# First self-attention of a two-layer decoder: the attention result is added to x by GpSimd, and its statistics are taken one tile later

## The reference, cut to what matters

```
q = x @ Wq.T;  k = x @ Wk.T;  v = x @ Wv.T          # 4 x 8 query heads, 8 key heads of 8 channels
probs = softmax(q k / sqrt(8))                      # per head, 64 x 64
a_dot = probs @ v
a_mem = (elu(q) @ memory) / (elu(q) @ memory_norm)
w = sigmoid(memory_weight)
out = a_dot * (1 - w) + a_mem * w
x = layernorm(x + out)                              # mean and variance over the 256 channels
```

## Time and profile before

| what | value |
|---|---|
| median of 3 runs | 1128.32 us (1126.15 to 1130.75) |
| the profiled execution's own time | 1124.46 us |
| its span, first to last instruction | 1122.7 us |
| busy over the span: PE, DVE, ACT, POOL | 87%, 50%, 32%, 17% |
| mean granted clock of TensorE | 0.927 |

### The profile page before, as it was taken

The page is one execution under the profiler, slowest core; times in us unless marked ns, Lnnn a source line. Parts: engine busy times, 40 slices in busy tenths (PEclk is TensorE's granted clock), DMA queues, the critical chain, the costliest instruction groups (busy, mean ns, idle before and its releaser), DMA issues.

```text
span 1122.7 us, 18938 instructions
## 1 busy us (share of the span) xinstructions
PE 976.7 (87%) x7488; PEld 610.0 (54%) x7488; DVE 556.4 (50%) x1121; ACT 358.9 (32%) x717; POOL 195.0 (17%) x233
## 2 busy tenths in 40 slices
PE   7998879998899999965763998889589999999994
PEld 4754523333478899962352567668354444444442
DVE  2699778885531101115687676357552323323325
ACT  3444336666222233322374453234211000000000
POOL 5010000000012222210036631060000111111110
PEclk9999869999899999997986999999578999999998
DMA  6000000000754555521001102030105022222001
GB/s 232 2 1 2 1 1 2 2 2 1 272 175 147 179 177 170 184 101 67 1 1 35 42 1 95 1 135 3 47 0 130 0 86 86 86 82 74 16 1 38
DMA packets 27210, 75.15 MB, mean 67 GB/s; under 512 B 9828, under 2 KB 17260, under 8 KB 21748
## 3 DMA queue, kind: packets, MB, share of 16 engines
q1 hardware_dynamic: 24916, 67.91, 17.9%
q0 software_dynamic: 2208, 6.03, 1.8%
HBM read 67.48 MB, written 6.46 MB: 66 GB/s over the span
## 4 chain that ended last, share of the span: by engine, by line
PE 70%; DVE 20%; issue 3%; ACT 3%; POOL 2%; DMA 1%; DVEq 0%; SPq 0%; POOLq 0%; ACTq 0%
PE psum L1508 8%; PE psum L1083 7%; PE psum L1095 7%; DVE arena L2048 4%; PE psum L806 3%; PE psum L1512 3%; PE psum L1274 3%; PE psum L1496 3%; PE psum L1538 2%; PE psum L1542 2%; PE psum L987 2%; PE psum L1474 2%; DVE arena L1974 2%; DVE arena L1973 2%; PE psum L1489 2%
## 5 line engine op out<-in xcount | busy, mean ns | idle before, releaser
L1508 PE MATMUL psum<-arena 128*128 128x512 f32 (+1 forms) x192 | 93.7, 625 | 0.5 <-DVE arena L2475 0.5
L1927 ACT ACTIVATE arena<-psum 128x512 f32<-128x512 f32 (+1 forms) x32 | 19.0, 593 | 227.3 <-PE psum L1512 227.3
L2048 DVE TENSOR_REDUCE arena<-psum 128x2 f32<-128x512 f32 x128 | 82.6, 687 | 15.5 <-PE psum L933 13.4
L1747 ACT ACTIVATE arena<-psum,arena 128x128 f32<-128x128 f32 x184 | 52.4, 367 | 115.5 <-PE psum L1083 91.0
L1083 PE MATMUL psum<-arena 128*128 128x128 f32 x736 | 86.8, 276 | 0.0
L1083 PEld LDWEIGHTS psum<-arena 128*128 128x128 f32 x736 | 84.0, 192 | 2.7 <-issue 2.7
L732 POOL TENSOR_TENSOR arena<-arena 128x512 f32<-128x512 f32 (+1 forms) x32 | 40.4, 1263 | 257.3 <-ACT arena L1927 257.3
L1095 PE MATMUL psum<-arena 128*128 x368 | 83.1, 379 | 0.0
L2195 DVE COPY arena<-psum 128x256 f32<-128x256 f32 x23 | 9.8, 425 | 135.7 <-PE psum L1068 85.3
L1724 ACT ACTIVATE arena<-psum 128x1024 f32<-128x1024 f32 x64 | 65.4, 1023 | 34.1 <-PE psum L955 31.0
L1095 PEld LDWEIGHTS psum<-arena 128*128 128x128 f32 x368 | 68.2, 190 | 8.4
(11 more groups left out here) (349 smaller groups left out, 1816.6 us busy)
## 6 DMA issues: line engine op xcount, KB each, us to landing
arena<-in_w SPq DMA_DIRECT2D x31, 1024.0 KB, 13.0
arena<-in_experts SPq DMA_DIRECT2D x8, 1248.0 KB, 6.3
arena<-mixed SPq DMA_DIRECT2D x16, 256.0 KB
arena<-mixed SPq DMA_DIRECT2D x8, 512.0 KB
arena<-in_ctx SPq DMA_DIRECT2D x2, 1024.0 KB, 7.2
arena<-returned SPq DMA_DIRECT2D x8, 256.0 KB, 4.2
arena<-in_w_xattn SPq DMA_DIRECT2D x1, 1538.5 KB, 9.9
arena<-in_w_ffn SPq DMA_DIRECT2D x1, 1152.0 KB, 5.3
```

The source lines that it names most:

```text
L1508: pe.matmul(out, e[w][:, k, :], xe6[:, half, k, :], start=(k == 0), stop=False)
L1747: last = act.activation(hidt[:, r % 2, ic * P:(ic + 1) * P], bank(n)[:, i * P:(i + 1) * P], ACT.Gelu, bias=b1_tile[:, r % 4, ic:ic + 1])
L2048: ax_max.by(dve.tensor_reduce(nmx[:, b % 2, :, h], bank(u % 2).rearrange("p (t s) -> p t s", t=2), AX.X, ALU.max, negate=True))
```

## The change

The division writes to two buffers in turn. GpSimd, after its eight additions of the memory part, goes through eight more, one for each divided tile, when `o0_read` says that it is there, and signals with the new semaphore `x0_ready`. VectorE no longer adds; in `finish0(j)` it takes the statistics of tile j - 1 instead of j, after a wait for GpSimd's addition of that tile, and those of tile 7 ahead of `normalise(0)`. From tile 2 on the division waits until GpSimd has read the buffer two tiles back. A later semaphore, `wd6_ps`, shares the new one's number.

```diff
-        t0 = arena.take(NQ * H0, DH0)
+        t0 = arena.take(2, NQ * H0, DH0)
...
+        x0_ready = signal("x0_ready")
...
-        wd6_ps = signal("wd6_ps")
+        wd6_ps = again("wd6_ps", x0_ready, NT)
...
                 xa_ready.by(pool.tensor_tensor(out=x[:, j, :], in0=x[:, j, :], in1=am[:, j % AM, :], op=ALU.add))
+            for j in range(NT):
+                pool.wait_ge(o0_read.sem, j + 1)
+                x0_ready.by(pool.tensor_tensor(out=x[:, j, :], in0=x[:, j, :],
+                                               in1=t0[:, j % 2, :, :].rearrange("p a b -> p (a b)"), op=ALU.add))
             pool.wait_ge(x_norm.sem, NT)
...
                 do(dve.reciprocal(rs0, src[:, :, DH0]))
-                do(dve.tensor_tensor(out=t0, in0=src[:, :, 0:DH0], in1=wide(rs0, 2, DH0), op=ALU.mult), o0_read)
-                dve.wait_ge(xa_ready.sem, j + 1)
-                do(dve.tensor_tensor(out=x[:, j, :], in0=t0.rearrange("p a b -> p (a b)"), in1=x[:, j, :], op=ALU.add))
+                if j >= 2:
+                    dve.wait_ge(x0_ready.sem, j - 1)
+                do(dve.tensor_tensor(out=t0[:, j % 2, :, :], in0=src[:, :, 0:DH0], in1=wide(rs0, 2, DH0), op=ALU.mult),
+                   o0_read)
+                if j >= 1:
+                    added_stats(j - 1)
+
+            def added_stats(j):
+                dve.wait_ge(x0_ready.sem, j + 1)
                 tile_stats(j)
...
                     finish0((b - 5) // 2)
+            added_stats(NT - 1)
             normalise(0)
```

## The result

| | before | after |
|---|---|---|
| executions | 12 | 12 |
| median, us | 1127.34 (1122.9 to 1130.75) | 1124.05 (1118.03 to 1129.71) |
| ratio to before | | 0.9954 (95% interval 0.9934 to 0.9974) |
| profiled execution's own time, us | 1124.46 | 1121.06 |
| its span, us | 1122.7 | 1119.2 |

The kernel became faster, by 3.3 us in the medians (a quotient of 0.9971) and by 2.9 to 7.4 in the interval of the ratio on record. That is clear of zero, but less than the 0.5% which the prediction called the least that such a measurement can tell.

The account below looks back on a forecast made before the run. VectorE was taken to pace the first self-attention up to the last softmax0, with a tail where only the last tile is late. 2.98 - 0.45 = 2.5 us gained, 1128.3 - 2.5 = 1125.8 us; range 1121.3 to 1129.8.

Parts of the forecast that it names:

- 5 x 0.46 + 0.68 = 2.98 us before T: Up to T, the last softmax0's end: five VectorE additions at 0.46 us and one 0.68 us statistics set drop out.
- TensorE keeps up, the lag of the first pair costs nothing: Sequence pairs before the last softmax0: TensorE keeps 0.6 us idle; its 0.8 us lateness counted as zero; rival's chance 0.10.
- The added waits find their signals set: VectorE's new waits for GpSimd's additions in finish0: signals already there, cost zero; if late, 0.64 us a tile.
- The tail grows by 0.45 us: After the last division, VectorE's last statistics wait for GpSimd's addition and its release: the tail 0.45 us longer.
- All of it reaches the end: From the first normalise on, signals start everything, so the whole 2.5 us gain should show in the total time.
- The additions block VectorE: Rival, in finish0: GpSimd's on-chip reads hold up VectorE's instructions beside them; 1.3 us slower, 1129.6 us; chance 0.05.
- The clock moves: Rival, cross-attention: TensorE's granted clock levels shift against the work, 1.0 to 3.0 us; chance 0.12 gain, 0.10 loss.
- 1125.8 us: Forecast total time: 1128.3 us, the median of three runs, less the 2.5 us gain; chance 0.60.

Follow-up runs that it names:

- e1: Kernel before the change, VectorE keeping the addition and only taking each tile's statistics one tile later; ratio 1.0003 to the kernel before.
- e3: The change, with VectorE also doing an equal addition into an unused scratch tile beside each GpSimd addition; ratio 0.9977 to the kernel before.
- e4: The change, with statistics moved to where VectorE waits for TensorE after the last softmax0; ratios 0.9958, 0.9954 and 0.9967 to the kernel before.
- e2: The change without the deferral: GpSimd adds, VectorE takes the same tile's statistics, waiting for each addition; ratio 1.0014 to the kernel before.
- e8: The change, with tile 7's statistics taken 4 more times ahead of the first normalise, 2.7 us; ratio 1.0017 to the kernel before.
- e9: The change, with one more set of statistics behind each of divisions 1 to 4, 2.7 us; ratio 1.0014 to the kernel before.
- the first two comparisons: The change run against the kernel before on two occasions, on different chips; ratios 0.9954 and 0.9964.
- e7: The change, with four more sets of statistics behind each of divisions 1 to 4, 10.9 us; ratio 1.0078 to the kernel before.

## Why the prediction was right

- *5 x 0.46 + 0.68 = 2.98 us before T.* Right: 2.95. e1 has the second term alone (0.67), e3 takes the first away again (2.27).
- *TensorE keeps up, the lag of the first pair costs nothing.* Right. It waits 0.68 us for VectorE in a pair, 0.6 was worked out; it is behind for one more pair than before, as was worked out too, and no softmax0 waits for it. Even e4, with pairs of 5.88 us, is not bound by it.
- *The added waits find their signals set.* Right; every gap of VectorE before T is 0.03 to 0.04 us. e2 is the price without the deferral.
- *The tail grows by 0.45 us.* It grew by 0.31 (the last L1953 starts 6.15 us after T, not 5.84). The release back to VectorE was taken from an addition of 512 columns, 0.21 us; here it takes 0.10. GpSimd's addition took 0.639 us, as its lines before had. The estimate of 0.55 us and a dispatch by the Trainium skill (GPSIMD Engine Reference, § 3.1) does not speak against that, but it leaves 0.09 us to a dispatch that it puts no number to.
- *All of it reaches the end.* Right: 2.64 us at the projection, 2.8 (0.5) in the whole at equal clock, and nothing left of it in e8 and e9.
- *The additions block VectorE.* It didn't happen: L1953 stayed at 426 to 429 ns beside them. The rule of the Trainium skill on two on-chip inputs (SBUF — State Buffer, § Who interferes with whom) is borne out by e3 against the change, 876 against 639 ns. The later instruction is 0.24 us longer there, while 0.39 us were left of the other; which part of each instruction reads on-chip memory the profile doesn't show. One reading in the prediction was off: L2010 takes 0.42 us and not 0.38, as its two in 0.76 us overlap. The argument stands, since all eight of them, with or without an addition beside them, take 0.414 to 0.425.
- *The clock moves*, by 1 to 3 us either way. The size was right for the cross-attention, but the cause was not: its length differs as much between profiles in which the projection starts at the same distance. For the whole the size was too small: from one execution to another the clock makes up to 7 us in one stage (213.0 and 219.7), and in the first two comparisons it added some 2 us to the change's gain.
- *1125.8 us.* The time by itself shows little. It was worked out from a median of three executions that was 1.0 us above the 1127.34 of the comparison, and the measured 1124.05 owes a part of its distance to the clock. That both came out inside the range is in part luck; the two distances carry the result.

## What to carry to other kernels

Work that is handed to an idle engine is free only if its consumer has something else to do meanwhile: the handover here is 0.82 us where the instruction itself had cost 0.50, so the offload and the deferral are one change, and either alone gains nothing or loses. When the stage's end is a tail on other engines, put the deferrable work into the waits of that tail rather than before it; that gave another 1.3 us. And for a gain of 0.2% read the distance between two events of the stage, which repeats to 0.02 us, and compare whole times at equal granted clock, as long as the kernels have about the same idle time.

## What the runs showed of the hardware

- Two instructions of 128x256 with two on-chip inputs each, VectorE's 0.04 us ahead of GpSimd's: VectorE's keeps its 0.43 us, GpSimd's goes from 0.64 to 0.88. Near 600 us, where the two engines run such instructions back to back, with other access patterns, VectorE's 128x256 takes 0.70 us and GpSimd's 128x220 0.65, more than its 128x256 here.
- GpSimd's end reaches a waiting VectorE in 0.10 us after 128x256 (e2 and the change), VectorE's end GpSimd in 0.07 to 0.09.
- TensorE at the granted clock of 1.00 ran its next turn at the low level behind 2.87 us of idle time (e7, 1.97 us in place of 1.09), and at the high one behind 1.35 us (e9) and 1.13 us (before).
- The mean granted clock of equal executions of the kernel before went from 0.915 to 0.931, and the time from 1133 to 1121 us with it.
